# Coefficients of a sparse code added in one plane before they are transposed, in a pipelined convolution and matching-pursuit kernel

## What is computed

```python
x = x + circular_conv3x3(groupnorm(x), weight)        # 64 -> 64 channels
x = x + sparse_code(groupnorm(x), dictionary)         # below
# sparse_code: every 4x4 patch of all 64 channels is one signal of 1024 numbers;
# the dictionary has 512 atoms of 1024 numbers, made unit length; G = D.T @ D
h = h_bar = D.T @ X
for k in range(5):
    index = argmax(abs(h), atoms not chosen before)    # one atom per signal
    # a row of a Cholesky factor from G[chosen, index]; then coefficients x_stack
    h = h_bar - x_stack @ G[chosen]
recon = D @ coeffs                                     # coeffs: 5 nonzeros of 512 per signal
```

## Time and profile before

| | |
|---|---|
| three runs | 4328.44 us median (4319.44 to 4348.53) |
| the profiled execution | 4336.29 us, of which the span from the first to the last instruction is 4334.6 us |
| PE busy | 3610.9 us (83%) |
| DVE busy | 2539.8 us (59%) |
| ACT busy | 1702.6 us (39%) |
| POOL busy | 1840.9 us (42%) |
| mean granted TensorE clock | 0.92 of full speed |

### The profile page before, as it was taken

How to read it: one execution, slowest core, us unless ns; L and a number is a source line. 1 busy time by engine, 2 the same in 40 slices (tenths; PEclk the granted TensorE clock), 3 DMA queues, 4 the chain that set the end, 5 groups by cost and what they waited for, 6 DMA issues and landing times.

```text
span 4334.6 us, 40291 instructions
## 1 busy us (share of the span) xinstructions
PE 3610.9 (83%) x10000; PEld 1751.4 (40%) x10000; DVE 2539.8 (59%) x6852; ACT 1702.6 (39%) x2771; POOL 1840.9 (42%) x1861
## 2 busy tenths in 40 slices
PE   6896888899888989889898898889789888986655
PEld 3343444444334434434343443444344443443322
DVE  2046566566555756656675665667566556756651
ACT  3434352444435343443534344353434435332211
POOL 0025444544444444444444444445445444535541
PEclk8998999999999999989999999999999999998878
DMA  2332343334334342433434243333424333332212
GB/s 98 116 121 85 90 114 100 111 80 128 96 91 114 101 119 76 120 96 98 111 101 129 67 129 89 96 109 107 124 66 129 95 93 106 94 85 57 56 44 39
DMA packets 253970, 420.51 MB, mean 97 GB/s; under 512 B 55696, under 2 KB 187024, under 8 KB 237200
## 3 DMA queue, kind: packets, MB, share of 16 engines
q0 software_dynamic: 91136, 202.10, 19.6%
q1 hardware_dynamic: 162576, 215.53, 15.3%
HBM read 281.18 MB, written 136.31 MB: 96 GB/s over the span
## 4 chain that ended last, share of the span: by engine, by line
PE 51%; DVE 15%; another core or an unknown queue 14%; issue 10%; ACT 6%; POOL 1%; DMA 1%; DVEq 1%; ACTq 0%; POOLq 0%
PE conv_ps L867 18%; PE gen_ps L829 17%; PE gen_ps L838 11%; PE ct_ps L802 5%; DVE idx L651 3%; DVE top L634 2%; DVE u L753 2%; ACT z L495 2%; DVE h L761 2%; DVE ce L576 2%; ACT score L542 2%; ACT xa L513 1%; ACT junk_sums L305 1%; POOL v L435 1%
## 5 line engine op out<-in xcount | busy, mean ns | idle before, releaser
L435 POOL DMA_INDIRECT v<-gram_rows,cell x1280 | 1253.4, 979 | 1280.0 <-DVE cell L657 913.5
L867 PE MATMUL conv_ps<-xh,wc 128*128 128x512 f32 x3072 | 1363.2, 599 | 32.7 <-ACT xa L513 17.8
L829 PE MATMUL gen_ps<-ct,dt 128*128 128x512 f32 x2048 | 964.4, 623 | 135.4 <-ACT ct L475 57.3
L838 PE MATMUL gen_ps<-dn,z 128*128 128x512 f32 x2048 | 912.0, 600 | 28.3 <-ACT z L495 20.0
L867 PEld LDWEIGHTS conv_ps<-xh,wc 128*128 128x128 f32 x3072 | 581.8, 192 | 753.7 <-issue 753.2
L802 PE MATMUL ct_ps<-ident,ce 128*128 128x128 f32 x2560 | 373.0, 304 | 446.5 <-DVE ce L576 288.0
L442 POOL DMA_INDIRECT u<-marked_rows,chosen x512 | 522.8, 1021 | 469.7 <-DVE chosen L661 317.9
L634 DVE MAX8 top<-score 128x8 f32<-128x512 f32 x640 | 419.6, 691 | 442.3 <-ACT score L542 332.2
L829 PEld LDWEIGHTS gen_ps<-ct,dt 128*128 128x128 f32 x2048 | 402.4, 200 | 648.2 <-issue 602.7
L576 DVE TENSOR_SCALAR ce<-count,which,xc 128x512 f32<-128x512 f16 x640 | 324.1, 554 | 542.4 <-remote 274.1
L838 PEld LDWEIGHTS gen_ps<-dn,z 128*128 128x128 f32 x2048 | 388.7, 192 | 514.7 <-issue 495.0
(11 more groups left out here) (93 smaller groups left out, 1323.3 us busy)
## 6 DMA issues: line engine op xcount, KB each, us to landing
xh<-x_skewed SPq DMA_DIRECT2D x128, 585.0 KB
xa<-x_pairs SPq DMA_DIRECT2D x64, 1024.0 KB, 7.7
y_rows<-xa SPq DMA_DIRECT2D x64, 1024.0 KB, 8.2
y_rows<-rb POOLq DMA_DIRECT2D x64, 1024.0 KB
v<-gram_rows,cell POOLq DMA_INDIRECT x1280
u<-marked_rows,chosen POOLq DMA_INDIRECT x512
dn<-atoms SPq DMA_DIRECT2D x1, 2048.0 KB, 8.8
gram_rows<-u SPq DMA_DIRECT2D x4, 256.0 KB, 2.0
```

The source lines that it names most:

```text
L435: pool.indirect_dma_start(v[:, g, k - 1, j, t:t + 1], None, cells, bass.IndirectOffsetOnAxis(ap=cell[:, g, k // (KMAX - 1), j, t:t + 1], a ...
L829: last = pe.matmul(to[:], dt_[:, a, d, :], ct[:, a, :], start=(a == 0), stop=(a == NA - 1))
L838: last = pe.matmul(to[:], z[:, t % 2, d // PATCH, d % PATCH, :], dn[:, d, :], start=(d == 0), stop=(d == ND - 1))
L867: last = pe.matmul(conv_ps[:, n], wc[:, m, :], xh[:, c % RING, n * CP + row:n * CP + row + CP, tap:tap + W], start=(m == 0), stop=(m == NT ...
```

## The change

It does five things. (1) The nonzeros of a tile are added on DVE in one plane. The plane of the first atom is made as before (TENSOR_SCALAR), and the other four are added to it by SCALAR_TENSOR_TENSOR, `one-hot * coefficient + plane`. The ring `ce` has two such planes. (2) The one-hots of those four are made by ACT in two activations of 512 columns each, `away = |which - count|` and `hot = relu(1 - away)`, in float16, with one buffer `away` and a ring of three for `hot`. (3) PE transposes one plane for each tile, in four transposes. (4) The hardware loop is gone: all 18 periods are written out, waits have constants, and no wait counts up a semaphore of its own. (5) The tables and PE's order are new, and x1 lies in `xa` by phase (even and odd row pairs apart), so that the store of x1 reads whole pieces of 8 KB in a partition in place of rows of 512 B.

```diff
-CE_RING = 4
+CE_RING = 2
+HOT_RING = 3
 # VECTOR_PLAN
-    1.5: [("co", 0)], 4: [("ce", 0, 0)], 5.5: [("ce", 0, 1)], 8.5: [("ce", 0, 2)], 9: [("ce", 0, 3)], 21: [("co", 1)],
-    22.5: [("ce", 1, 0)], 25.5: [("ce", 1, 1)], 29: [("ce", 1, 2)], 31.5: [("ce", 1, 3)],
+    1: [("co", 0)], 3.5: [("ce", 0, 0)], 5: [("ce", 0, 1)], 8.5: [("ce", 0, 2)], 9.5: [("ce", 0, 3)],
+    23.5: [("co", 1)], 24: [("ce", 1, 0)], 25.5: [("ce", 1, 1)], 29.5: [("ce", 1, 2)], 31.5: [("ce", 1, 3)],
 # SCALAR_PLAN, two of its new lines
+    3: [("z", 4), ("oh", 0, 0, 1), ("oh", 0, 0, 2), ("oh", 0, 0, 3), ("oh", 0, 0, 4), ("oh", 0, 1, 1),
+        ("oh", 0, 1, 2), ("z", 5), ("ev", 0), ("oh", 0, 1, 3)],
+    31: [("re", 0, 6), ("ct", 1, 0), ("oh", 1, 3, 3), ("ct", 1, 1), ("oh", 1, 3, 4), ("re", 0, 7), ("ct", 1, 2),
+        ("ct", 1, 3), ("ev", 7), ("st", 16), ("st", 17), ("re", 1, 0), ("rt", 1)],
 # ACT
+                elif kind == "oh":
+                    act.wait_ge(which_ready[g], at(img, KMAX, j + 1))
+                    ...
+                    act.activation(away[:], count[:], ACT.Abs, bias=which[:, img % 2, g, j, t:t + 1], scale=-1.0)\
+                        .then_inc(hot_step, 1)
+                    act.wait_ge(hot_step, at(img, 2 * TILES * (KMAX - 1), 2 * m + 1))
+                    if not (first and m < HOT_RING):
+                        tile, step = divmod(m - HOT_RING, KMAX - 1)
+                        act.wait_ge(ce_step, at(img, TILES * KMAX, tile * KMAX + step + 2))
+                    act.activation(hot[:, m % HOT_RING, :], away[:], ACT.Relu, bias=plus_minus[:, 0:1], scale=-1.0)\
+                        .then_inc(hot_step, 1)
 # DVE
-                        dve.tensor_scalar(ce[:, place, :], count[:], which[:, parity(img), g, j, t:t + 1], xc[:, g, j, t:t + 1],
-                                          ALU.is_equal, ALU.mult).then_inc(ce_ready, 1)
+                            dve.tensor_scalar(ce[:, place, :], count[:], which[:, img % 2, g, 0, t:t + 1], coef,
+                                              ALU.is_equal, ALU.mult).then_inc(ce_step, 1)
+                        else:
+                            m = n * (KMAX - 1) + j - 1
+                            dve.wait_ge(hot_step, at(img, 2 * TILES * (KMAX - 1), 2 * m + 2))
+                            dve.wait_ge(ce_step, at(img, TILES * KMAX, n * KMAX + j))
+                            dve.scalar_tensor_tensor(ce[:, place, :], hot[:, m % HOT_RING, :], coef, ce[:, place, :],
+                                                     ALU.mult, ALU.add).then_inc(ce_step, 1)
 # PE
-                for j in range(KMAX):
-                    pe.wait_ge(ce_ready, at(img, TILES * KMAX, n * KMAX + j + 1))
-                    ...
-                        last = pe.matmul(ct_ps[:, a, :], ce[:, place, a * P:(a + 1) * P], ident[:], is_transpose=True,
-                                         start=(j == 0 and a == 0), stop=(j == KMAX - 1), skip_group_check=True)
+                pe.wait_ge(ce_step, at(img, TILES * KMAX, (n + 1) * KMAX))
+                if not (img == 0 and n == 0):
+                    pe.wait_ge(ct_ready, at(img, TILES, n))
+                for a in range(NA):
+                    last = pe.transpose(ct_ps[:, a, :], ce[:, n % CE_RING, a * P:(a + 1) * P], ident[:])
+                last.then_inc(ce_turned, 1)
 # PE's order at the end of the coefficients (after)
+                    recon(i, 0, 6)
+                    recon(i, 0, 7)
                     turn(i - 2, 1, 1)
+                    turn(i - 2, 1, 2)
+                    turn(i - 2, 1, 3)
+                    recon(i, 1, 0)
 # and the convolution's rounds 2 and 3 stand one behind the other
 # layout
-        def phase(g, ph):
-            return slice(g * PAIRS // GROUPS + ph, (g + 1) * PAIRS // GROUPS, PHASES)
+        def place(g, ph):
+            return quarter(g * PHASES + ph)
```

More of the change, by code:

```diff
@@ L46 @@
 HW = ATOMS + 8
-FIRST = 4
 GN_EPS = 1e-5
@@ L118, in lag @@
         return 0 if n < T else 1
-    return 2 if kind in ("co", "ce", "ct", "re") else 0
+    return 2 if kind in ("co", "oh", "ce", "ct", "re") else 0
 def bank_of(what):
     return [what in bank for bank in BANKS].index(True)
[L126 to L150, removed]
 def at(image, per_image, n):
-    if isinstance(image, int):
-        return image * per_image + n
-    return image.turn * (2 * per_image) + (image.n * per_image + n)
+    return image * per_image + n
 def preact_conv_pursuit(nc, x, skewed, w_taps, atoms, ident_in, avg_in, out):
@@ L189, in preact_conv_pursuit @@
         ce = sb("ce", [P, CE_RING, ATOMS])
+        hot = sb("hot", [P, HOT_RING, ATOMS], F16)
+        away = sb("away", [P, ATOMS], F16)
         ct = sb("ct", [P, NA, T * P])
@@ L351, in statistics, with parts @@
                                bias=shifted[n][:, 0:1]).then_inc(gn_step[n], 1)
[L353 to L365, removed]
-            return {back: loop or 0 <= i - back < images for back in (-1, 0, 1, 2)}
+        def parts(i):
+            return {back: 0 <= i - back < images for back in (-1, 0, 1, 2)}
         def first_loads(sp):
@@ L409, in period @@
                         g = r // (ROUNDS // GROUPS)
-                        stop_until(x1_ready, at(i, ROUNDS, r + 1))
+                        sp.wait_ge(x1_ready, at(i, ROUNDS, r + 1))
                         for ph in range(PHASES):
                             if here[1]:
-                                stop_until(x1_out[g * PHASES + ph], at(i, 16, 0))
-                            sp.dma_start(out[number(i)][g, ph], xa[par][:, phase(g, ph), :])\
+                                sp.wait_ge(x1_out[g * PHASES + ph], at(i, 16, 0))
+                            sp.dma_start(out[i][g, ph], xa[par][:, place(g, ph), :])\
                                 .then_inc(x1_out[g * PHASES + ph], 16)
-            periods(sp, period)
+            for i in range(images + 2):
+                period(i, i % 2)
             for n in range(GROUPS * PHASES):
@@ L459, in period @@
                             add(i - 2, *what)
-            periods(pool, period)
+            for i in range(images + 2):
+                period(i, i % 2)
         @block.scalar
@@ L523, in root, with period @@
                 act.activation(gsc[n][:, 4:5], gsc[n][:, 3:4], ACT.Sqrt).then_inc(gn_root[n], 1)
-            def period(i, par, loop=False):
-                here = parts(i, loop)
+            def period(i, par):
+                here = parts(i)
                 for n, (back, g, k) in enumerate(UNITS):
-                    img = apart(i - back, g)
+                    img = i - back
                     for t in range(T):
@@ L547, in _ @@
             root(0, 0)
-            periods(act, period)
+            for i in range(images + 2):
+                period(i, i % 2)
         @block.vector
         def _(dve):
-            def stop_until(sem_, value):
-                dve.wait_ge(sem_, value)
-                dve.sem_inc(vector_passed, 1)
             def extra(what, i, par, back):
@@ L784, in period @@
                             between(s)
-                    search(apart(i - back, g), g, k, between)
+                    search(i - back, g, k, between)
             for part in (1, 2, 3):
                 gn_part(0, 0, 0, part)
-            periods(dve, period)
+            for i in range(images + 2):
+                period(i, i % 2)
         @block.tensor
@@ L955, in _ @@
             bias(0, 0)
-            periods(pe, period)
+            for i in range(images + 2):
+                period(i, i % 2)
 def setup(nc, ctx, sem, w_taps, atoms, ident_in, avg_in, gram, marked, dn, dt_, taps, tap_sum, h, u, count, ident, avg,
```

217 lines of the change are left out of this document (105 added, 112 removed), and 35 rows, old and new, of tables (BANKS, SCALAR_PLAN, VECTOR_PLAN).

## The result

In a first series of runs the changed kernel took 4198.7 us (median of 4, 4175.5 to 4213.3) where the kernel before took 4333.9: a ratio of 0.968, 95% interval 0.965 to 0.972. Forecast were 4045. The gain is there and less than half of what I had said; the time is at the upper end of the range.

A forecast was written before the change was run, and what follows sets the result against it. PE was taken to bound the kernel, 83% busy, losing mainly at the coefficient handshake. Its period would fall from 252.0 to 231.5 us, 14 times 20.5 = 287 less, giving 4045 us; range 3850 to 4200.

The forecast's parts named there:

- convolution rounds: PE's convolution rounds 2 and 3 now stand together and wait 1.39 us a period.
- slow clock and rest: PE's first matmuls behind a wait run at a lower rate: 10 us a period before, 8 after.
- the handshake: PE's transposes waiting for coefficient planes, 25.1 us a period: 17 behind search (0, 3) stay, the other 8 go.
- The transposes: On PE, 160 transposes a period become 32, 14.0 us less.
- The turns in succession: On PE, three tiles in succession cost a copy each: 2.4 us a period, up to 3 x 3 where ACT is late.
- the drain behind the last full period: After period 15: more DVE work, fewer handshakes; taken as 0 us, bounds -40 and +20.
- Rival (b): In-order coupling: ACT and DVE wait for each other, 10 us a period, giving 4181 us; chance 0.15.
- ScalarE's 64 activations: One-hots on ACT at 0.61 + 0.03 us each, 41 us a period, bounds 33 and 42.
- DVE comes out level with PE: DVE at 230 to 240 us a period, with little to win below 226 unless its other waits shrink.
- The loop, the fetches and the layout: Writing out the loop, PE's instruction fetches and x1's layout by phase: no effect on the time.
- Rival (a): The slow stretch under POOL's gather streams goes with the handshake: 3908 us, or 3770 if DVE's waits shrink; chance 0.27.
- rival (c): Slower: group 1's one-hots fall into slow stretches, 1.2 us for each signal that does, 4540 us; chance 0.06.

The follow-up runs named there:

- series 1: First series, disturbed: the changed kernel against the kernel before, 4198.7 us against 4333.9, ratio 0.968.
- series 5: Quiet series: the changed kernel as it is against the kernel before, 3709.2 us, ratio 0.981.
- series 4: Disturbed series: the changed kernel as it is against the kernel before, 3970.3 us, ratio 0.925.
- a_narrow: Changed kernel with one-hots 8 columns wide in place of 512 after the first image, against the changed kernel: 4114.0 us against 4151.0.
- b_flat: Kernel before with only its hardware loop written out, against the kernel before: ratio 0.9994, in a quiet series.

## Why the prediction was wrong

A period in us, by the terms of the forecast:

```
                         forecast   series 1   quiet (series 5)
PE's work                  195.7      195.7       195.7
turns                       19.4        6.2         5.1
reconstruction                -        16.9         0.8
convolution rounds           1.4        7.3         3.0
other waits                  7          2.9         0.0
slow clock and rest          8         13.1         5.7
sum                        231.5      242.1       210.3
(the kernel before                    252.0       216.3)
```

The step that failed is the one on the handshake: "I take it that these 17 stay, and that the other 8 go". The first half was right in size and wrong in place: 17 us a period stayed, not at the turns behind search (0, 3) but before the third reconstruction, behind the stream of units (1, 4) and (0, 2), the longest one in the new order. The second half was wrong: the other 8, and the part of the slow clock that I let go with them, belonged to the disturbance like the 17, as the quiet run of the kernel before shows with 0.8 us of waits at its transposes. They did not go with the handshake: in series 1 the convolution rounds wait 7.3 where I had 1.4 (5.1 of it stands as "issue", which the quiet run does not have), and the slow clock and rest are 13.1 where I had 8. I had seen the disturbance in the earlier trace rows and still priced a third of its damage as a cost of the handshake. The sum of the forecast took 20.5 us from a period. The change by itself takes 6.0; the other 3.9 of the 9.9 in series 1 come of a disturbance that hit the changed kernel for 31.8 us and the kernel before for 35.7. That difference is no property of the change that I can show: in series 4 it was far larger.

Point by point. The transposes: 14.0 us less, right, and the only gain there is. The turns in succession: 2.4 was forecast (up to 9 "where ACT is late"); it is 6.2 in series 1 and 5.1 quiet, since the last of them waits 2.2 to 3.7 us for its plane, a wait that the sum did not have. The convolution: 1.4 for one pair of rounds; the quiet run has 3.0, as three of a period's rounds wait 0.65 to 1.4 us for ScalarE's copy. In quiet runs all of PE's waits rise from 3.6 to 8.9 us a period and the slow clock and rest from 3.0 to 5.7, and these 8.0 of the 14.0 are given back. Outside the periods the change loses too: the drain behind the last full period takes 365 us in the quiet profile and 349 in that of the kernel before, where I had taken 0 (bounds -40 and +20). So of 14 x 6.0 = 84 us the quiet runs keep 71. Rival (b), in-order coupling, which I had at 10 us and a chance of 0.15, gives 4181, nearest to the 4199 measured. Waits of its kind are there, but its price for each one-hot is not shown, and in series 1 the larger part of the miss is the disturbance, so the nearness is partly luck.

ScalarE's 64 activations were taken at 0.61 + 0.03; a pair repeats every 1.56 us:

```profile
2368.32 0.72 ACT L447 ACTIVATE away<-count,which 128x512 f16<-128x512 f16 x1
2369.07 0.72 ACT L454 ACTIVATE hot<-away,plus_minus 128x512 f16<-128x512 f16 x1
2369.88 0.72 ACT L447 ACTIVATE away<-count,which 128x512 f16<-128x512 f16 x1
```

64 of them are 49.9 us, beyond my bound of 42. The row I took had no bias operand, and these have one. A run of the same activation with and without it was not made. The Trainium skill, ScalarE: Activation LUTs, section on what ACT_TABLE_LOAD costs, states this: 186 ns and 0.833 a column with immediate scale and bias, about 93 more with a bias read from a [128, 1] tile; from these I estimate 612 and 706 for 512 columns. The trace agrees, 610 for `score` and 710 to 722 here. The 8 us would not have moved the forecast much: in `a_narrow` some 26 us a period less of ScalarE's time were worth 2.6 us.

DVE: the size of the addition was right, "DVE comes out level with PE" wrong. Of the 59 us of other idle time that I kept for it, about 13 were the disturbance: the kernel before has 46 in the quiet run. The changed kernel idles 45 in all there, in a period of 210, well under my 226. The loop, the fetches and the layout at nothing: `b_flat` confirms the first two, the layout was not tried alone. (That 1.35 MB are all of PE's instructions was misread: written out, with the same number of PE's instructions, the queue brings 0.97 MB.) Rival (a), the stretch goes with the handshake, is refuted for series 1, and when the stretch goes of itself, it goes for both kernels. Of rival (c) there is a little: in 9.9 periods of series 1 DVE's additions waited 87 times for a one-hot, 107.8 us in all, and in twelve quiet periods 37 times, 20.8 us; the kernel was still faster than before. The Trainium skill's warning of dense completion increments (VectorE: DVE Perf Modes, section on the TRN2 errata) is not enough to explain the stretch: the changed kernel has the same increments in quiet and disturbed series, and only the latter have the stretch.

What stays open is what makes a series disturbed, and whether long streams of gathers are a condition of the stretch: the trial that would decide it, all streams broken, never met a disturbed series. That the changed kernel gained 3.2, 3.8 and 7.5% in the three disturbed series is open too; in series 4 its period was 226 us, with more slow small operations of DVE than in series 1 (72 against 53) but less waiting of PE beside them.

## What to carry to other kernels

A wait in one profile has a cause that may not be the program's. Before a wait is priced as what a change can win, take the kernel before a second time, on another chip and at another time. Here that would have shown the handshake at nothing, and the forecast's own terms would have left 14.0 - 2.4 - 1.4 = 10.2 us a period: 4336.3 - 14 x 10.2, less 8, is about 4185 in place of 4045. When five signals are replaced by a chain through a third engine in order, plan the order anew: in quiet series the same operations were 2% faster than before in one order and 11% slower in another.

## What the runs showed of the hardware

Disturbed series: for a whole series the kernel before ran 13 to 15% longer (4291 to 4334 us against 3779 to 3781), with unchanged instructions and data, the changed kernel 7 to 13% (3970 to 4199 against 3709), and the same operations in the order of before 2% (4307 against 4204). In the slow stretches a chain of small operations of DVE has 1.22 to 1.24 us between two where 0.04 is usual in the quiet rows above, and PE's matmuls of one reconstruction come every 2.8 us. In the changed kernel's two profiles of series 1 and 4 such operations lie 21 to 40 us behind the first gather of a stream of 28, apart from two, and end within 5 us of its last. TensorE's granted clock from 1000 to 3400 us, a mean of its two levels (1.2 and 2.4 GHz), was 1.00 in the quiet run of the kernel before, where PE waited 3.6 us a period, and 0.94 in its disturbed one with about 32. Making POOL wait for a landing cost 1.3 us a wait with 18 of them in a period and 2.9 with four.
